# Graph attention on one core: the row maximum over the partitions by one GpSimd operation per block, in place of four TensorE transposes and what stood between them

## The reference

```
h = max(layernorm(x), 0)                 # x: 4096 x 256
q, k, v = h @ Wq.T + bq, h @ Wk.T + bk, h @ Wv.T + bv
a = q @ k.T / sqrt(256) + adj + adj      # 4096 x 4096
out = x + softmax(a, axis=-1) @ v
```

## Time and profile before

| what | before |
|---|---|
| median of three runs | 813.82 us |
| the profiled execution | 813.86 us, its span 812.1 us |
| PE busy | 804.3 us (99%) |
| DVE, POOL, ACT busy | 589.2, 383.9, 361.1 us |
| share of PE in the chain that ended last | 96% |
| longest wait of PE after its start | 1.8 us |
| one exponential tile of 128x512 on ACT | 605 ns |

### The profile page before, as it was taken

How to read it: one execution, slowest core, us unless ns; L and a number is a source line. 1 busy time by engine, 2 the same in 40 slices (tenths; PEclk the granted TensorE clock), 3 DMA queues, 4 the chain that set the end, 5 groups by cost and what they waited for, 6 DMA issues and landing times.

```text
span 812.1 us, 16621 instructions
## 1 busy us (share of the span) xinstructions
PE 804.3 (99%) x6708; PEld 802.3 (99%) x6708; DVE 589.2 (73%) x982; ACT 361.1 (44%) x651; POOL 383.9 (47%) x333
## 2 busy tenths in 40 slices
PE   8999999999999999999999999999999999999998
PEld 8999999999999999999999999999999999999998
DVE  6868777776777777777777767777776777777754
ACT  6683443334344434444443444444344434444365
POOL 4546736072633708264280825528082551818273
PEclk9999999999999999999999999999999999999999
DMA  8521433243333324323333333323333332333300
GB/s 266 178 83 55 116 91 109 75 131 92 92 111 91 111 78 125 98 85 112 92 107 90 106 103 92 118 82 110 95 104 105 91 106 82 114 104 93 91 27 14
DMA packets 43997, 81.68 MB, mean 101 GB/s; under 512 B 5009, under 2 KB 5905, under 8 KB 43921
## 3 DMA queue, kind: packets, MB, share of 16 engines
q1 hardware_dynamic: 43344, 79.84, 33.4%
q10 hardware_dynamic: 576, 0.79, 0.3%
HBM read 76.42 MB, written 4.19 MB: 99 GB/s over the span
## 4 chain that ended last, share of the span: by engine, by line
PE 96%; DVE 1%; ACT 1%; POOL 1%; DMA 1%; issue 0%; ACTq 0%; DVEq 0%; POOLq 0%
PE ps L335 49%; PE ps L437 15%; PE ps L438 15%; PE ps L439 15%; PE ps L327 1%; DMA w_all<-in_w 1%; PE ps L412 0%; PE ps L419 0%; ACT x_pair L515 0%; DVE x_third L618 0%; POOL v L289 0%; PE ps L346 0%; POOL rstd L275 0%; ACT v_full L533 0%; ACT hT L505 0%
## 5 line engine op out<-in xcount | busy, mean ns | idle before, releaser
L335 PE MATMUL ps<-qhl,hT 128*128 128x256 f32 x3072 | 406.1, 282 | 0.0
L335 PEld LDWEIGHTS ps<-qhl,hT 128*128 128x128 f32 x3072 | 383.2, 190 | 0.0
L306 POOL TENSOR_TENSOR ring_a<-ring_a,m_row 128x512 f32<-128x512 f32 x179 | 230.5, 1330 | 211.5 <-ACT m_row L584 211.5
L437 PE MATMUL ps<-v,p_hi 128*128 128x258 f32 x1024 | 292.1, 285 | 0.3 <-DVE p_lo L675 0.3
L438 PE MATMUL ps<-v,p_lo 128*128 128x258 f32 x1024 | 289.0, 282 | 0.0
L439 PE MATMUL ps<-v,p_hi 128*128 128x256 f32 x1024 | 288.5, 282 | 0.0
L580 ACT CAST p_hi<-ps 128x512 fp32r<-128x512 f32 x256 | 150.6, 588 | 246.8 <-PE ps L439 244.5
L641 DVE TENSOR_TENSOR ring_a<-ps,ring_a 128x512 f32<-128x512 f32 x179 | 123.4, 689 | 101.3 <-PE ps L335 100.4
L437 PEld LDWEIGHTS ps<-v,p_hi 128*128 128x128 f32 x1024 | 194.6, 190 | 0.5 <-DVE p_lo L675 0.5
L438 PEld LDWEIGHTS ps<-v,p_lo 128*128 128x128 f32 x1024 | 193.9, 189 | 0.0
L439 PEld LDWEIGHTS ps<-v,p_hi 128*128 128x128 f32 x1024 | 193.2, 189 | 0.0
(11 more groups left out here) (76 smaller groups left out, 358.3 us busy)
## 6 DMA issues: line engine op xcount, KB each, us to landing
ring_a<-in_adj SPq DMA_DIRECT2D x179, 256.0 KB, 2.7
ring_b<-in_adj SPq DMA_DIRECT2D x77, 256.0 KB, 2.7
x_res<-in_x SPq DMA_DIRECT2D x16, 256.0 KB, 3.0
out<-x_res SPq DMA_DIRECT2D x15, 256.0 KB, 2.0
x_pair<-in_x SPq DMA_DIRECT2D x5, 512.0 KB, 4.0
x_third<-in_x SPq DMA_DIRECT2D x2, 512.0 KB, 4.7
w_all<-in_w ACTq DMA_DIRECT2D x3, 256.0 KB, 4.3
x_pair<-in_x SPq DMA_DIRECT2D x4, 128.0 KB, 2.9
```

Source lines behind the costliest of these rows:

```text
L306: nc.gpsimd.tensor_tensor(slot_tiles(w), slot_tiles(w), m, ALU.subtract).then_inc(s_sub, 1)
L335: last = nc.tensor.matmul(dst, lhs(a, ib), rhs(c, ib), start=(n == 0), stop=(n == 3 * DB - 1))
L437: nc.tensor.matmul(ps[:, at, 0:VW], hi, v[:, n, 0:VW], start=(n == 0), stop=False)
```

## The change

The four transposes, the fold of the transposed maxima, the spread and ACT's copy go. DVE writes the joined maxima to `key_max`. POOL takes the maximum over the partitions with one operation, `partition_all_reduce`, and has it on all partitions in `m_row`. POOL then adds the row term and takes it away again, with two operations of 128x256. For this the row terms are needed as a row on all partitions. They are turned by DVE in blocks of 32x32 (`turn_terms`, two instructions in all), written to DRAM (`spill_terms`, eight small DMAs in all) and read back by a DMA that puts 256 of them on each partition (`load_terms`, one per block).

```
+            def spill_terms(n):
+                sp.wait_ge(s_turn, n + 1)
+                for c in range(P // 32):
+                    sp.dma_start(term_spill[n][:, 32 * c:32 * c + 32], terms_turned[32 * c:32 * c + 32, n])\
+                        .then_inc(s_tst[n], 16)
+
+            def load_terms(b):
+                n = 0 if QS * b < GT * EARLY_GROUPS else 1
+                sp.wait_ge(s_tst[n], 16 * (P // 32))
+                if b > 0:
+                    sp.wait_ge(s_m, b)
+                sp.dma_start(term_row[:, :], bass.AP(term_spill[n].tensor, b * QB, [[0, P], [1, QB]])).then_inc(s_tin, 16)
...
+            def maximum(b):
+                pool.wait_ge(s_cols, b + 1)
+                if b > 0:
+                    pool.wait_ge(s_sub, UNITS * b)
+                nc.gpsimd.partition_all_reduce(m_row[:, :], key_max[:, :], P, bass.bass_isa.ReduceOp.max).then_inc(s_max, 1)
+                pool.wait_ge(s_max, b + 1)
+                pool.wait_ge(s_tin, 16 * (b + 1))
+                nc.gpsimd.tensor_tensor(m_row[:, :], m_row[:, :], term_row[:, :], ALU.add).then_inc(s_shift, 1)
+                pool.wait_ge(s_shift, b + 1)
+                nc.gpsimd.tensor_tensor(m_row[:, :], m_row[:, :], term_row[:, :], ALU.subtract).then_inc(s_m, 1)
+                pool.wait_ge(s_m, b + 1)
...
                 if u == 0:
-                    pool.wait_ge(s_m, b + 1)
+                    maximum(b)
...
-                if u == 0 and b <= BLOCKS:
-                    turn_max(b - 1)
-                if u == 1 and b <= BLOCKS:
-                    spread_max(b - 1)
...
-            def keep_max(b):
-                act.wait_ge(s_bcast, b + 1)
-                nc.scalar.copy(m_row[:, b % 2], ps[:, X_BANK, 0:QB]).then_inc(s_m, 1)
...
                     if b > 0:
-                        dve.wait_ge(s_bcast, b)
+                        dve.wait_ge(s_max, b)
-                    halves = acc[:, :].rearrange("p (k i n) -> p k i n", k=KT, i=QS)
-                    nc.vector.tensor_tensor(max_rows[:, :, :], halves[:, 0], halves[:, 1], ALU.max)\
-                        .then_inc(s_cols, 1)
+                    halves = acc[:, :].rearrange("p (k q) -> p k q", k=KT)
+                    nc.vector.tensor_tensor(key_max[:, :], halves[:, 0], halves[:, 1], ALU.max).then_inc(s_cols, 1)
...
+            def turn_terms(n, groups):
+                dve.wait_ge(s_vhi, 2 * groups)
+                nc.vector.transpose(terms_turned[:, n], row_terms[:, n]).then_inc(s_turn, 1)
...
-                if u == 1 and b <= BLOCKS:
-                    reduce_max(b - 1)
+                if s == FIRST + 1:
+                    turn_terms(1, GROUPS)
```

More of the change, by code:

```diff
@@ L37, in graph_attention_kernel @@
     VW = D + 2
+    EARLY_GROUPS = 5
+    term_spill = [nc.dram_tensor(f"term_spill{n}", [TILES, P], f32, kind="Internal").ap() for n in range(2)]
     ctx = ExitStack()
@@ L53, in graph_attention_kernel @@
         acc = sb("acc", [P, BANK])
[L54 to L58, removed]
+        key_max = sb("key_max", [P, QB])
+        m_row = sb("m_row", [P, QB])
+        term_row = sb("term_row", [P, QB])
+        row_terms = sb("row_terms", [P, 2, TILES])
+        terms_turned = sb("terms_turned", [P, 2, TILES])
         query_bias = sb("query_bias", [P, DB])
@@ L174, in graph_attention_kernel @@
         s_cols = sem("key_halves_joined")
-        s_turn = sem("max_turned")
-        s_red = sem("row_max_reduced")
+        s_tz = sem("row_terms_zeroed")
+        s_turn = sem("row_terms_turned")
+        s_tst = [sem(f"row_terms_spilled{n}") for n in range(2)]
+        s_tin = sem("term_row_loaded")
+        s_max = sem("max_over_partitions")
         s_shift = sem("row_max_shifted")
-        s_rows = sem("row_max_spread")
-        s_bcast = sem("row_max_broadcast")
         s_m = sem("row_max_in_rows")
@@ L238, in _ @@
                 load_adj(s)
+            spill_terms(0)
+            load_terms(0)
+            spill_terms(1)
             sp.wait_ge(s_vlo, 2 * GROUPS)
@@ L247, in _ @@
                     store(b - 1)
+                if u == 1 and b + 1 < BLOCKS:
+                    load_terms(b + 1)
                 if u == 4:
@@ L264, in _ @@
             nc.gpsimd.memset(ones[:, :], 1.0)
+            nc.gpsimd.memset(row_terms[:, :, :], 0.0).then_inc(s_tz, 1)
             nc.gpsimd.memset(v[:, :, D:VW].bitcast(f32), 1.0).then_inc(s_const, 1)
@@ L303, in _ @@
                 if u == 0:
-                    pool.wait_ge(s_m, b + 1)
-                m = m_row[:, b % 2].rearrange("p (one q) -> p one q", one=1).broadcast_to([P, KT, QB])
+                    maximum(b)
+                m = m_row[:, :].rearrange("p (one q) -> p one q", one=1).broadcast_to([P, KT, QB])
                 nc.gpsimd.tensor_tensor(slot_tiles(w), slot_tiles(w), m, ALU.subtract).then_inc(s_sub, 1)
@@ L373, in project_q @@
             def project_q(b):
-                if b >= 2:
-                    pe.wait_ge(s_red, b - 1)
                 for ob in range(DB):
@@ L403, in scores @@
                 last.then_inc(s_score, 1)
[L405 to L420, removed]
             def weigh_values(w):
@@ L531, in v_hi @@
                 t = GT * g + 2 * pair
+                if t == 0:
+                    act.wait_ge(s_tz, 1)
                 at = ps[:, v_bank(g, pair):v_bank(g, pair) + 2, :]
@@ L534, in v_hi @@
                 nc.scalar.copy(v[:, t:t + 2, 0:D], at[:, :, 0:D])
-                nc.scalar.activation(row_terms[:, t:t + 2], at[:, :, D], ACT.Identity, bias=term_bias[:, :],
+                nc.scalar.activation(row_terms[:, 0 if g < EARLY_GROUPS else 1, t:t + 2], at[:, :, D], ACT.Identity, bias=term_bias[:, :],
                                      scale=QSCALE).then_inc(s_vhi, 1)
@@ L589, in _ @@
                     write_p_hi(due(s) + 1)
-                if u == 1 and b <= BLOCKS:
-                    keep_max(b - 1)
                 if s not in HOLD and 0 <= due(s) + 2 < STEPS:
@@ L749, in _ @@
                 running_max(2 * g)
+                if g == EARLY_GROUPS:
+                    turn_terms(0, EARLY_GROUPS)
             add_adj(FIRST - 1)
```

## The result

The changed kernel takes 827.83 us (median of four runs, 827.29 to 829.69) against 813.84. The ratio is 1.0174 with a 95% interval of 1.0161 to 1.0187: slower by about 14 us. The forecast was 825.8 us, in a range of 809 to 865. The profiled execution took 827.29 us, its span is 825.5.

What follows compares the result with a forecast made beforehand. PE, busy 804.3 of 812.1 us, was taken as the bound: 813.86 - 7.8 (transposes) + 13.2 (block 0) + 4.2 (last block) + 2.3 (PE slow after a wait) = 825.8 us, range 809 to 865.

Steps and rivals of the forecast that it cites:

- What bounds the kernel: Whole kernel: PE, busy 804.3 of 812.1 us, sets the time; other engines' work costs only by coming late.
- The gain: PE without transposes: 0.44 us a block, 6.6 us over fifteen blocks, and 1.24 us in the last; 7.8 us in all.
- L: Time from the fold's end on DVE to `m_row`: reduction 2.6, library load 5.5, row-term operations and waits 1.6; 9.7 us.
- Middle blocks free: Middle blocks: `m_row` may come 12.2 us after the fold, so 9.7 us fits with 2.5 to spare, costing nothing.
- Block 0: Block 0: both loads and the reduction queue on POOL behind the last `v_lo`; `m_row` at 88.9, PE waits 13.2 us.
- Last block: Last block: 5.5 us of room from the fold to `m_row`, 9.7 us needed; costs 4.2 us.
- PE after a long wait: PE behind block 0's 13 us wait: slow as at its start, 2.3 us charged once; bounds 0 and twice that.
- Rival 1: Library loads on POOL cost near 0.01 us; block 0 waits 2.2 us, last block nothing: 808.3 us; chance 0.17.
- Rival 2: Reduction plus load above 10.6 us makes every middle block wait, 14 us per microsecond over; 877 us worked out; chance 0.22.
- Rival 3: POOL becomes the bound, the reduction taking 39 us: 74 us a block against 46, some 1270 us; chance 0.03.

Runs made afterwards that it cites:

- no_switch: Changed kernel with POOL's reduction replaced by an elementwise addition, so no library load; maximum over the partitions left out: 807.7 us, ratio to before 0.9921.
- middle_five_more: Changed kernel with five reductions more in each of the 14 middle blocks: 895.53 us, ratio to before 1.1014.
- loads_alone: As no_switch, but POOL loads the other library ahead of the wait for the partial maxima and the standard one behind it: 826.94 us, ratio to before 1.0157.
- first_block_old: Changed kernel with block 0's maximum made by the transposes of before, the other 15 by the new operation: 812.94 us, ratio to before 0.9991.

## Why the prediction was right

The time came within 2 us of the forecast. Each cost was looked for in the right place. That the number is so close is in part luck, for errors in several sizes cancel: the gain came out 1.7 us smaller than forecast, the two waits 0.65 and 0.7 us shorter, and what the clock costs behind them 1.1 us more, which leaves the 1.5 us by which the profiled execution (827.29) missed 825.8.

- *What bounds the kernel.* Right. PE's two waits, the slow products behind them and the transposes make up the whole difference, but for tenths.
- *The gain, 7.8 us.* Too high by 1.7, or by 1.4 if the waits are counted by starts. The price of a transpose was right (0.109 us measured against 0.11). But plain steps came out 0.005 us longer, so a block gave 0.35 us. The last block gave 1.10 by the table and 1.26 by starts, for 1.24. At the start the whole run begins 0.25 us later, which hid part of what block 0 saved: PE waits 1.76 us for `ident` where it waited 1.51. It is 1.76 or 1.77 in every kernel with library loads and 1.51 in every one without.
- *L, 9.7 us.* Measured 9.9, by luck. The reduction takes 1.09 us where I took 2.6 from four elementwise passes. The load behind it takes 7.2 us (115.3 us of idle time over 16) where I took 5.5 from the slowest DMA. Both were guesses from rows of other work, one too high by 1.5 and the other too low by 1.7. No run shows the 5.5 us behind the reduction, or that a load is a transfer: the DMA queues of kind instruction moved 78 packets in the changed kernel and 77 in no_switch, which loads nothing at the 16 maxima. What they show in its place is idle time of POOL, 6.85 to 7.69 us behind each of the 16 reductions. The one ahead of the reduction takes 5.65. The two operations on the row terms take 1.5 to 1.6, as said.
- *Middle blocks free.* Right, with 13.1 us of room where I worked out 12.2; most of the difference is that `p_lo` starts 2.66 us after `m_row` there (139.25 to 141.91) and not 3.25. Which wait ends last there (`finish`) was right too.
- *Block 0, 13.2 us.* Measured 12.55. `m_row` came at 89.1 for 88.9, again because the reduction and the second load cancel. From `m_row` to the first product it took 3.5 us where I took 3.95, and PE was ready at 80.0 and not at 79.6.
- *Last block, 4.2 us.* Measured 3.49, for the most part because of the same 3.5 us.
- *PE after a long wait, 2.3 us once.* The term that was mis-sized. It came twice, 1.56 and 2.5 us. Of the second, 0.6 came back: before, the next product also began late, for a `p_lo` that stood behind `finish` in DVE's queue, and that delay went. The net is 1.56 + 1.85 = 3.4 us for the 2.3 charged. A wait of 3.5 us was enough to bring the clock down; I had charged nothing there.
- *Rival 1, cheap switches.* Fallen: no_switch shows about what it would have given, 807.7 us, against 808.3 worked out. The one load that spoke for it, at the start, left at most 0.24 us of idle time ahead of POOL's next instruction, and 0.50 in the changed kernel, where the 32 new ones cost 5.65 to 7.7 each wherever they can be seen. Its side remark, that loads of up to 2.5 us stay at or under the time before, is off by its own figures: 7.2 + 1.2 is 8.4 us of waits against 7.8 gained.
- *Rival 2, middle blocks wait.* Did not happen, but middle_five_more shows that it is the cliff it was said to be, and a steeper one: 4.8 us a block for 2.9 us too late.
- *Rival 3, the reduction at 39 us.* Far off; 1.09 us.

## What to carry to other kernels

An operation of GpSimd may be cheap and the way to it dear: here the reduction took 1.09 us, and each library load next to it, where it could be seen, 5.6 to 8.3 us of the queue (the shortest and the longest idle time before such an instruction in all runs), invisible as busy time and paid where the result was awaited. Work out the room at the first and the last turn of a pipeline apart from the middle: here the middle had 13 us of room, needed 10 and lost nothing, while the two ends lost 19.5. And price a wait of TensorE by more than its length: the granted clock fell to 0.50 in or right behind waits of 2.75 to 12.6 us here, and the waits of 12.55 and 3.49 us cost 14.1 and 5.3 us in all. Where a wait can't be avoided, filler matmuls are worth a try; here they gave back 3.3 us.

## What the runs showed that was not expected

- The load behind the reduction takes longer (6.9 to 7.7 us) than the one ahead of it (5.65 us in block 0, the only block where it can be seen; 5.6 to 6.2 over the runs), with or without the reduction (6.8 to 7.5 and 5.63 us in loads_alone).
- The maximum over 128 partitions of 256 columns takes 1.085 us, left on all of them, against 0.73 us of an elementwise operation of that size. Made again it costs about the same: five more in a row take 6.03 us, 1.2 us each with the wait between them.
- The same wait does not always cost the same. In the last block of the changed kernel the granted clock was 0.50 when the first product began. In first_block_old, after a wait of 3.6 us, it was still 1.00, and only then it fell (0.54 from 784 to 786): the first seven of the product's twelve matmuls ran at full speed, and the slow ones cost 1.6 us and not 2.5. In block 0 of loads_alone, after a wait of 12.2 us, the clock stayed at 0.50 from 92 to 98, over the first product and the scores, and that cost 2.7 us where the changed kernel lost 1.56.
